# Where a feed-forward block issues the mask units: between its two products, or in front of both

## What is computed

```python
mask = adjacency_matrix.astype(jnp.float32) + jnp.eye(n, dtype=jnp.float32) > 0
for l in range(attn_w.shape[0]):                      # three layers
    si = x @ attn_w[l, :d]
    sj = x @ attn_w[l, d:]
    scores = si[:, :, None] + sj[:, None, :] + attn_b[l]
    scores = jnp.where(scores >= 0, scores, 0.2 * scores)
    scores = jnp.where(mask, scores, -jnp.inf)
    attn = jax.nn.softmax(scores, axis=-1)
    agg = jnp.einsum('bij,bjd->bid', attn, x)
    h = layernorm(x + agg, g1[l], beta1[l])
    ff = jax.nn.gelu(h @ W1[l] + b1[l], approximate=False) @ W2[l] + b2[l]
    x = layernorm(h + ff, g2[l], beta2[l])
...
Wh = jnp.matmul(h, W)                                 # the graph-attention layer
e = jax.nn.leaky_relu(e_i[:, :, None] + e_j[:, None, :], negative_slope=ALPHA)
attention = jax.nn.softmax(jnp.where(adj == 0, MASK_VAL, e), axis=2)
out = jax.nn.elu(jnp.matmul(attention, Wh))
```

## Time and profile before

| what | value |
| --- | --- |
| time, median of three executions | 2446.71 us (2444.73 to 2447.41) |
| the profiled execution | 2446.48 us, span 2444.8 us |
| mean granted TensorE clock | 0.986 of full speed |
| busy: PE, VectorE, ScalarE, GpSimd | 92%, 77%, 64%, 47% of the span |
| chain that ended last, by engine | PE 61%, VectorE 26%, issue 5%, GpSimd 4%, ScalarE 3%, DMA 1% |

### The profile page before, as it was taken

The page is one execution under the profiler, slowest core; times in us unless marked ns, Lnnn a source line. Parts: engine busy times, 40 slices in busy tenths (PEclk is TensorE's granted clock), DMA queues, the critical chain, the costliest instruction groups (busy, mean ns, idle before and its releaser), DMA issues.

```text
span 2444.8 us, 41401 instructions
## 1 busy us (share of the span) xinstructions
PE 2254.4 (92%) x14623; PEld 1711.6 (70%) x14623; DVE 1892.5 (77%) x5043; ACT 1572.0 (64%) x2450; POOL 1139.1 (47%) x2128
## 2 busy tenths in 40 slices
PE   5889999998899999999899999999998999999988
PEld 4666766776667767767777767777675777677667
DVE  7777778758788887888887788978878677767875
ACT  5467566666666676676766666766656557666754
POOL 3344346354264543644546444554544445335643
PEclk9899999999999999999999999999999999999989
DMA  6312012011130112200121102111131010010000
GB/s 217 120 44 90 6 61 78 11 51 48 48 113 1 44 48 83 78 19 26 64 84 61 44 5 91 60 53 44 40 108 56 6 44 10 5 40 23 23 25 29
DMA packets 66221, 128.55 MB, mean 53 GB/s; under 512 B 12985, under 2 KB 53213, under 8 KB 62942
## 3 DMA queue, kind: packets, MB, share of 16 engines
q1 hardware_dynamic: 66014, 125.90, 15.4%
HBM read 111.20 MB, written 14.68 MB: 51 GB/s over the span
## 4 chain that ended last, share of the span: by engine, by line
PE 61%; DVE 26%; issue 5%; POOL 4%; ACT 3%; DMA 1%; SPq 0%; DVEq 0%; POOLq 0%; ACTq 0%
PE OB L1639 40%; PE FBB L1639 13%; DVE mj L1250 5%; DVE pw L1274 4%; PE RB L1639 4%; DVE gT L1288 3%; DVE st L1141 2%; DVE junk L1192 2%; PE TH L1639 2%; DVE xc L1168 1%; DVE junk L1197 1%; PE TH L1680 1%; POOL xc L676 1%; DVE xc L1155 1%; DMA adjst<-in_adj 1%
## 5 line engine op out<-in xcount | busy, mean ns | idle before, releaser
L1639 PE MATMUL OB<-xx,pw 128*128 128x257 f32 x4096 | 947.2, 386 | 22.7 <-DVE xc L1168 10.9
L1639 PEld LDWEIGHTS OB<-xx,pw 128*128 128x128 f32 x4096 | 770.3, 192 | 149.9 <-DVE xc L1168 16.8
L1639 PE MATMUL FBB<-hT,wb 128*128 128x512 f16 x2304 | 563.1, 383 | 55.1 <-DVE gT L1288 54.3
L1639 PE MATMUL OB<-wb,gT 128*128 128x256 f16 x4608 | 572.4, 275 | 10.1 <-DVE gT L1288 10.1
L1639 PEld LDWEIGHTS OB<-wb,gT 128*128 128x128 f16 x4608 | 453.4, 99 | 141.3 <-DVE gT L1288 12.6
L649 POOL TENSOR_SCALAR ve<-mv 128x2 f32<-128x2 f32 x256 | 59.5, 233 | 1026.5 <-DVE mv L1144 1018.1
L891 ACT ACTIVATE FBB<-FBB,wc 128x512 f32<-128x512 f32 x384 | 252.2, 657 | 292.3 <-PE FBB L1639 291.7
L1639 PEld LDWEIGHTS FBB<-hT,wb 128*128 128x128 f16 x2304 | 214.0, 98 | 265.7 <-DVE gT L1288 66.6
L1288 DVE TENSOR_TENSOR gT<-FBB,gT 128x512 f16<-128x512 f32 x384 | 262.0, 683 | 171.9 <-ACT gT L896 171.7
L902 ACT ACTIVATE pw<-pw,sj 128x512 f32<-128x512 f32 x512 | 334.1, 710 | 59.7 <-DVE pw L1274 58.9
L676 POOL TENSOR_TENSOR xc<-xc,gb 128x256 f32<-128x256 f32 x384 | 292.0, 760 | 33.5 <-ACT xc L866 32.4
(11 more groups left out here) (141 smaller groups left out, 2334.0 us busy)
## 6 DMA issues: line engine op xcount, KB each, us to landing
wb<-w_scratch SPq DMA_DIRECT2D x19, 2048.0 KB, 7.9
adjst<-in_adj SPq DMA_DIRECT2D x56, 512.0 KB, 4.1
xx<-in_x SPq DMA_DIRECT2D x16, 512.0 KB, 5.7
nm<-in_L_gnn_W SPq DMA_DIRECT2D x6, 1024.0 KB, 8.5
gb<-in_L_gnn_g SPq DMA_DIRECT2D x48, 128.0 KB, 2.8
adjst<-in_x SPq DMA_DIRECT2D x6, 1024.0 KB, 10.9
out_x<-adjst SPq DMA_DIRECT2D x48, 128.0 KB, 1.7
pw<-in_adj SPq DMA_DIRECT2D x4, 1024.0 KB, 9.6
```

The source lines that it names most:

```text
L1639: return pe.matmul(o, lhsT, rhs, start=first, stop=last)
```

## The change

In a step with a feed-forward block, `prepare(k, 8 + n)` on TensorE no longer issues the units of the turn; a new function, `units_of`, issues them between `hidden(k, n + LAG)` and `second(k, n)`. The transposes and spreads of `prepare`, the units of graph-attention steps, those in the aggregation and those of point END stay where they are. At n = 14 and 15 there is no `hidden`, so the units stand in front of `second` as before. No other engine's code is changed.

```diff
--- before.py
+++ after.py
@@ -1844,7 +1844,12 @@
                     spread_s1(k + 1)
                 if tabs["sj"] == at:
                     spread_sj(k + 1)
-                for u in tabs["units"].get(at, ()):
+                if is_gat(k) or at == END or at < NT:
+                    units_of(k, at)
+
+            def units_of(k, at):
+
+                for u in prep_tables(k)["units"].get(at, ()):
                     unit(k + 1, u)
 
             def ffn_step(k):
@@ -1889,6 +1894,7 @@
                         gat_colsum(SUM_AT[k])
                     if n + LAG < NF:
                         hidden(k, n + LAG)
+                    units_of(k, 8 + n)
                     second(k, n)
                 prepare(k, END)
```

## The result

The changed kernel takes 2452.45 us (median of 9 runs, 2449.71 to 2456.51), the kernel before 2446.49 beside it (9 runs, 2439.65 to 2447.70). The ratio is 1.0039, with a 95% interval of 1.0028 to 1.0049: slower by more than the 0.2% that can be told from nothing. The medians lie 6.0 us apart, the ratio says 9.5 (7 to 12); forecast were 8. All ratios leave out two executions that stood far above the rest of their kernels: 6131.99 us with the late edges and 2674.50 us, at a granted clock of 0.845, in the control. The profiled execution took 2452.89 with a span of 2451.2, 6.4 above that of before.

The account below looks back on a forecast made before the run. TensorE, busy 92% of the span, was taken as the bound. Terms -6.4 + 7.6 + 2.2 + 1.5 + 2.25 + 0.8 = +7.95 on 2446.48 gave 2454.4 us, range 2450 to 2460, chance 0.62.

Parts of the forecast that it names:

- Ahead steps, -6.4: Steps 9, 13, 17, 21: hidden products fill the waits before units; each step 1.6 us shorter, -6.4 in all.
- Up to n = 9, +1.25 a block: Graph-attention blocks: unit behind hidden(7) +0.15, late scores delaying gat_low +0.8 at n = 7, +0.3 at n = 9.
- The gain of turn 4 is lost: Step 8 and its like: second(4) starts 1.1 us earlier, but the following transpose still waits for gat_low, so none stays.
- The tail, +1.0 - 0.35: End of graph-attention blocks: late scores of units 13 and 14 delay the aggregation 1.0 us; earlier exponentials give back 0.35.
- step 24 +2.2: Step 24, which had no unit wait, loses 2.2 us by the same terms as step 8.
- The wait for the residual adds: Profile sign: grown by 0.5 us or more in steps 2, 8, 12, 16, 20, 24 to 26.
- Steps 2, 25, 26, +0.75 each: Same block end without graph attention; VectorE's 0.28 us of idle before the residual adds leaves 0.75 of 1.0, +2.25 in all.
- Step 28, +1.5: Step 28, VectorE's queue full at the end: late scores 1.25 us, block end 0.6, less 0.35.
- The tail is taken up: Rival, chance 0.23: the next aggregation absorbs the late block ends; total +0.4 us, 2446.9, no change.
- Faster: Rival, chance 0.09: VectorE's run before gat_low shortens with TensorE's lead, keeping turn 4's 1.1 us in five steps; -11.1, 2435.4.
- The clock rival: Rival, chance 0.06: waits in step 8 and its like tip TensorE to a lower clock in five steps; +8.5 more, 2462.9.
- Strict order: VectorE takes its queue first-in, first-out; if a correction could pass a waiting score, +1.25 and the block-end term would be zero.

Follow-up runs that it names:

- the late edges: Changed kernel with VectorE's last edge operations of step 28 (n = 13) issued behind the score columns of turn 15; ratio 1.0043 to the kernel before.
- the control: Kernel before, with only VectorE taking gat_low ahead of the turn's scores; 2438.97 us, ratio 0.9983.
- the first kernel of single turns: Kernel before, other turns moved in each of five blocks (step 16: n = 12 and 13; step 28: n = 4 to 8); ran once, 2450.31 us.
- the kernel of graph-attention steps: Kernel before, with units in the new place only in steps 8, 12, 16, 20, 24 and 28; 2456.99 us, ratio 1.0059.

## Why the prediction was right, and where it was not

It forecast slower by 8 us for the reasons that were then found, with one term far too small. Measured term by term the loss is near 11, so that the forecast lies inside the 7 to 12 of the ratio partly because that interval is wide.

- *Ahead steps, -6.4.* Measured -1.56 each in every kernel with the new place there, -6.25.
- *Up to n = 9, +1.25 a block.* Turns 2 to 8 alone: +1.25. Its parts were sized 0.15, 0.8 and 0.3; in the changed kernel's timeline the transposes of n = 5, 7 and 9 start 0.0, 0.82 and 1.23 late. By single turns, 0.65 and 0.18 come from late scores (turns 6 and 8) and 0.42 from single units that no longer pass while gat_low ends (turns 5 and 9; the one of turn 7 costs nothing). I had the second cause only at n = 5, and put the rest down to late scores.
- *The gain of turn 4 is lost* at the transpose behind gat_low: shown, +0.03 a block.
- *The tail, +1.0 - 0.35.* In step 8 the aggregation starts 2.07 late, 0.82 more than the 1.25, and ends its first part 1.75 late: +0.8 and -0.3. Moving turns 12 and 13 by themselves (step 16 of the first kernel of single turns) starts the scores of units 13 and 14 0.93 late, as forecast, but the residual adds only 0.64 late: VectorE's unbroken run between them took 4.33 instead of 4.62, since its first two score columns took 0.79 and 0.41 instead of 0.43 and 0.93. The aggregation gives 0.33 back, and 0.31 are left of the 0.65. Four blocks: +7.6 forecast, +6.97 measured; step 24 +2.2 and +1.91. The wait for the residual adds grew from 0.19 to 0.53 in steps 2, 8, 12, 16, 20, 25 and 26 and not at all in step 24, where 0.5 or more was forecast for all of them.
- *Steps 2, 25, 26, +0.75 each.* Block and aggregation together +0.58, +0.46 and +0.58, 1.6 in all for 2.25.
- *Step 28, +1.5: the term that was mis-sized.* The block is 6.96 longer; the aggregation behind it starts 62.77 after the block's start instead of 57.03: +5.7. The prediction took its late scores to cost what they cost in step 8 and saw the full queue only at the end. In fact VectorE has next to nothing from turn 9 on that could take up a late score: behind the waits of 1.04 and 1.19 for units it is 3.7 late at the pair of scores at 2300.99, and still 3.7 at the edges. Step 8 is 3.7 late at that pair too, but only 2.1 at its residual adds: it had 0.58 and 1.48 of idle in front of its last corrections, step 28 only the 0.58. On top, the edge operations take 1.55 longer, so that the residual adds come 5.5 late; and TensorE goes to half clock behind its wait of 3.69. What the clock adds is small: in the kernel of graph-attention steps, with the same wait but less of that slow stretch, the aggregation still starts 5.0 late.
- *What hid the error.* The terms as measured are -6.25 + 6.97 + 1.91 + 5.7 + 1.6 and some 0.8 of single turns in steps 11, 15, 23, 27 and 4, near +11, inside the 7 to 12 of the ratio. The profiled pair shows 6.4: the block of step 0 was 2.2 shorter after than before, and the stretch behind the start of step 28's aggregation, where no instruction moved, took 129.5 instead of 131.7 (see the last section).
- *Rivals.* "The tail is taken up" is wrong for the changed kernel (0.5 of 0.65 remains). "Faster", by gat_low that ends sooner, is not what happened; but when VectorE is given that order by hand, it is the cure. The clock rival's step 8 kept its 1.00. The drop came behind the longest wait, in step 28: a granted clock of 0.62 over 9 us, between full 2.4 and 1.2 GHz, with the 24 matmuls of the last two products at 5.29 us where they took 2.78 in step 8 of the kernel before. That agrees with the Trainium skill (TensorE: Matmul & The Clock Gate, "Why this matters for your kernels"), which warns of pauses between bursts.
- *Strict order.* Nothing passed a waiting score: the one at 773.13 waited 1.84 with gat_low behind it, whose only input, the transposition begun at 766.81 for 0.63, was long there; put ahead of the score by hand, gat_low ran earlier. That agrees with what the Trainium skill (TensorE: Matmul & The Clock Gate, "Architectural detail: the array is 16× 32×32, not 1× 128×128") states of VectorE.

## What to carry to other kernels

Moving a producer a little later in the bounding engine's queue is free there as long as it filled no wait (two that did cost 0.42 us a block), but every consumer that takes its queue in order now waits at that place, with all that stands behind it: list what does, and move it ahead of the wait (here one swap was worth 1.9 us a block, 0.5 of it without the change too). The price of a late result depends on the idle time left in the consumer's queue from there to its next deadline, so price the busiest instance of a repeated block by itself: the moved units of turns 9 to 11 cost at most 0.4 us in steps 12 and 16, and 3.5 in step 28. Apply such a change only to the blocks where the trace shows the wait that it is to fill.

## What was not expected of the hardware

- Stretches at half clock fall differently from one execution to the next, in parts with the same instructions. The block of step 0 took 64.40 us before, 62.17 after, 62.38 with only the ahead steps changed, and 64.43 with only the graph-attention steps changed, which have the old order there both; the mean granted clock over it was 0.89 in the two long ones and 0.92 in the two short ones. The block of step 1 took 51.34 before, at 0.97, and 49.70 with the graph-attention steps changed, at 1.00. A difference of 2 us between two profiled spans says nothing until the blocks have been compared.
- The eight edge operations of VectorE (128x128 each) took 2.19 us in step 8 before, 3.07 in step 28 before, and 4.62 in step 28 after. GpSimd was busy for 1.27 of the 3.07 and for 3.56 of the 4.62, with operations of 128x256 elements; in step 8 it was busy for 1.22 of the 2.19, with operations of 128x2. Its busy share alone doesn't order the three. This was seen, not isolated: no run here changed GpSimd's work alone. The Trainium skill (SBUF — State Buffer, "Terms") says that VectorE and GpSimd arbitrate for a shared pair of ports, the loser blocked for the whole instruction; the two rows of step 28 agree with it in direction, and no run here shows that it is the cause.
